# One query and key projection over exchanged halves, copied to both halves of the partitions by ScalarE

## What is computed

```python
x = _ln(x, ln1_w, ln1_b)                      # x: 8 batches of 512 tokens, 256 wide
qk = _silu(x @ Wqk.T + bqk)                   # 64 wide
v = _silu(x @ Wv.T + bv)                      # 512 wide
heads = qk[..., None, :] * gamma + beta       # four heads out of the one qk
quad_q, lin_q, quad_k, lin_k = map(_rope, (heads[..., i, :] for i in range(4)))
# _rope(h): x1, x2 = the two halves of h (32 wide each)
#           concatenate([x1 * cos - x2 * sin, x2 * cos + x1 * sin])
quad_att = einsum(quad_q, quad_k) / G + bias  # within groups of 64 tokens
lin_kv = einsum(lin_k, v) / n                 # over a batch
out = gate * (relu(quad_att)**2 @ v + lin_q @ lin_kv)
```

## Time and profile before

| | us |
|---|---|
| median of 3 runs | 1041.61 |
| lowest, highest | 1039.89, 1043.02 |
| profiled execution, its own time | 1043.68 |
| span of the profiled execution | 1041.6 |
| PE busy | 956.5 (92%) |
| DVE busy | 732.5 (70%) |
| ACT busy | 542.7 (52%) |
| attention block (until the experts' first instructions) | 347 |

### The profile page before, as it was taken

The page is one execution under the profiler, slowest core; times in us unless marked ns, Lnnn a source line. Parts: engine busy times, 40 slices in busy tenths (PEclk is TensorE's granted clock), DMA queues, the critical chain, the costliest instruction groups (busy, mean ns, idle before and its releaser), DMA issues.

```text
span 1041.6 us, 17866 instructions
## 1 busy us (share of the span) xinstructions
PE 956.5 (92%) x6060; PEld 846.2 (81%) x6060; DVE 732.5 (70%) x1671; ACT 542.7 (52%) x956; POOL 258.6 (25%) x246
## 2 busy tenths in 40 slices
PE   4979999999997899968999999999999999999971
PEld 3767788788876799957999999999999989999861
DVE  6697878787875663235666666666666678998596
ACT  5535555655455444433555555555555566666425
POOL 0050000000000037770111111112221156665551
PEclk9989999999998999998999999999999999999976
DMA  4424436533233734524344333344334436555706
GB/s 159 111 102 112 114 85 167 150 102 76 81 127 113 233 127 140 182 90 167 123 148 139 120 122 122 128 154 144 133 133 131 143 123 209 189 195 196 241 22 222
DMA packets 77426, 145.23 MB, mean 139 GB/s; under 512 B 10146, under 2 KB 61343, under 8 KB 70848
## 3 DMA queue, kind: packets, MB, share of 16 engines
q1 hardware_dynamic: 66864, 124.06, 37.4%
q0 software_dynamic: 6816, 16.86, 4.6%
q10 hardware_dynamic: 3696, 3.67, 1.0%
HBM read 99.59 MB, written 45.76 MB: 140 GB/s over the span
## 4 chain that ended last, share of the span: by engine, by line
PE 42%; DVE 9%; POOL 7%; issue 4%; DMA 2%; ACT 1%; DVEq 0%; SPq 0%; POOLq 0%
PE bank L1450 20%; PE bank L1491 20%; POOL slot_rows L1091 6%; DVE s_hl L1373 2%; PE bank L1476 2%; DMA k_wstage<-wall 1%; PE bank L1447 1%; DVE k_wpj1l L1301 1%; DVE s_wpj0l L1301 1%; DVE s_rows L1343 1%; DMA s_rows<-expert_results 1%; DVE s_mst L1351 1%; DVE s_acc L1331 0%; ACT s_h L1157 0%; DMA s_xb<-slot_rows 0%
## 5 line engine op out<-in xcount | busy, mean ns | idle before, releaser
L1157 ACT ACTIVATE s_h<-bank,k_bfc 128x512 f32<-128x512 f32 (+1 forms) x248 | 155.6, 627 | 273.5 <-PE bank L1491 243.4
L1373 DVE TENSOR_TENSOR s_hl<-s_h,s_hh 128x512 fp32r<-128x512 f32 (+1 forms) x248 | 168.1, 679 | 184.5 <-ACT s_hh L1161 183.5
L1098 POOL DMA_INDIRECT expert_results<-s_y,s_dest x78 | 85.7, 1099 | 322.5 <-ACT s_y L1138 305.7
L1491 PE MATMUL bank<-k_uh,k_wfc1h 128*128 128x512 f32 (+1 forms) x480 | 151.0, 364 | 1.2 <-DVE k_uh L1370 0.7
L1161 ACT ACTIVATE s_hh<-s_h 128x512 fp32r<-128x512 f32 (+1 forms) x248 | 141.4, 570 | 10.7
L1450 PE MATMUL bank<-k_wpj1l,s_hh 128*128 128x256 f32 x464 | 130.8, 282 | 1.5 <-DVE s_hl L1373 1.5
L1450 PE MATMUL bank<-k_wpj1h,s_hh 128*128 128x256 f32 x464 | 130.5, 281 | 0.0
L1450 PE MATMUL bank<-k_wpj1h,s_hl 128*128 128x256 f32 x464 | 130.4, 281 | 0.0
L1450 PE MATMUL bank<-s_wpj0l,s_hh 128*128 128x256 f32 x384 | 109.1, 284 | 7.7 <-DVE s_hl L1373 7.7
L1450 PE MATMUL bank<-s_wpj0h,s_hh 128*128 128x256 f32 x384 | 109.2, 284 | 0.0
L1450 PE MATMUL bank<-s_wpj0h,s_hl 128*128 128x256 f32 x384 | 108.9, 284 | 0.0
(11 more groups left out here) (284 smaller groups left out, 2288.5 us busy)
## 6 DMA issues: line engine op xcount, KB each, us to landing
k_wstage<-wall SPq DMA_DIRECT2D x50, 1024.0 KB, 5.2
slot_rows<-s_empty SPq DMA_DIRECT2D x6, 1677.0 KB, 11.5
s_xb<-slot_rows SPq DMA_DIRECT2D x15, 516.0 KB, 4.0
s_rows<-expert_results SPq DMA_DIRECT2D x12, 512.0 KB, 7.4
s_x_in<-x SPq DMA_DIRECT2D x8, 512.0 KB, 3.5
s_x_res<-x SPq DMA_DIRECT2D x8, 512.0 KB, 11.0
x_rows<-s_x SPq DMA_DIRECT2D x8, 512.0 KB, 2.8
x_parts<-s_x1h SPq DMA_DIRECT2D x8, 512.0 KB, 2.6
```

Of the source, the lines that this page charges most:

```text
L1098: pool.indirect_dma_start(YY, bass.IndirectOffsetOnAxis(dest[i][:, t:t + 1].bitcast(U32), 0), y[:, t, :], None, bounds_check=2 * N - 1, oo ...
L1157: nc.scalar.activation(h[j % 2][:, cols], b[:, cols], ACT.Gelu_apprx_tanh, bias=bfc[w][:, j:j + 1]).then_inc(h_ev, 1)
L1373: tt(hl[j % RING][:, cols], h[j % 2][:, cols], hh[j % RING][:, cols].bitcast(F32), ALU.subtract).then_inc(hl_rd, 1)
L1491: last = mm(b[:, cols], wfc[w][ws][:, c, rows_], xs[i][:, c, cols], start=c == 0 and p == 0, stop=c == KD - 1 and p == 2)
```

## The change

The projection is made once: its 128 columns are qk (partitions 0 to 63) and halves(qk) (partitions 64 to 127), in bank 4. ACT reads each half of the partitions and writes it to both halves of `qk[:, s, :]`: four activations of 64 partitions each, in place of two of 128. DVE's first rope multiplication waits for the first two of them, its second for all four. The one product now waits for both things for which the two products waited: `u_ml` (bank 4's former reader) and `x1T_ev` (bank 5's). Bank 5 keeps only its other uses. The weights shrink from 512 to 256 values a partition, so their load and their two splitting instructions shrink too.

```diff
-        wqk, wv, wg, wo = (pair(n, s) for n, s in (("wqk", [P, 2, KD, P]), ("wv", [P, KD, E]),
+        wqk, wv, wg, wo = (pair(n, s) for n, s in (("wqk", [P, KD, P]), ("wv", [P, KD, E]),
...
-        raw_qk = raw[:, 2048:2560].rearrange("p (s k n) -> p s k n", s=2, k=KD)
+        raw_qk = raw[:, 2048:2304].rearrange("p (k n) -> p k n", k=KD)
...
                 if main:
+                    act.wait_ge(q_mm, b + 1)
                     for s in range(2):
-                        act.wait_ge(q_mm, 2 * b + s + 1)
                         need(act, qkr_rd, 2 * (b - 1) + s + 1)
-                        nc.scalar.activation(qk[:, s, :], bank[4 + s][:, :], ACT.Silu,
-                                             bias=vec[:, BQK + s:BQK + s + 1]).then_inc(q_ev, 1)
+                        src = slice(s * QK, (s + 1) * QK)
+                        for dst in (slice(0, QK), slice(QK, P)):
+                            nc.scalar.activation(qk[dst, s, :], bank[4][src, :], ACT.Silu,
+                                                 bias=vec[src, BQK + s:BQK + s + 1]).then_inc(q_ev, 1)
...
                     for s in range(2):
-                        dve.wait_ge(q_ev, 2 * b + s + 1)
+                        dve.wait_ge(q_ev, 4 * b + 2 * s + 2)
...
                 if main:
-                    for s in range(2):
-                        if at(0):
-                            pe.wait_ge(wl_rd, 2)
-                        if s == 0:
-                            need(pe, u_ml, 4 * b)
-                        else:
-                            need(pe, x1T_ev, 2 * (c - 1) + 2)
-                        for k in range(KD):
-                            last_i = three(bank[4 + s][:, :], wqk[0][:, s, k, :], wqk[1][:, s, k, :], xTh[:, k, :], xTl[:, k, :],
-                                           k == 0, k == KD - 1)
-                        last_i.then_inc(q_mm, 1)
+                    if at(0):
+                        pe.wait_ge(wl_rd, 2)
+                    need(pe, u_ml, 4 * b)
+                    need(pe, x1T_ev, 2 * (c - 1) + 2)
+                    for k in range(KD):
+                        last_i = three(bank[4][:, :], wqk[0][:, k, :], wqk[1][:, k, :], xTh[:, k, :], xTl[:, k, :], k == 0, k == KD - 1)
+                    last_i.then_inc(q_mm, 1)
...
     wqk = f[A + "Wqk"].T
-    wqk = np.stack([chunks(np.concatenate([w, w], 1)) for w in (wqk, halves(wqk))], 1)
+    wqk = chunks(np.concatenate([wqk, halves(wqk)], 1))
```

## The result

The changed kernel takes 1052.93 us (median of 4 runs, 1049.41 to 1054.31) against 1040.75 of the kernel before, measured beside it (4 runs, 1039.2 to 1043.02): a ratio of 1.0099, 95% interval 1.0082 to 1.0116. It is slower by some 10 to 12 us where the prediction had it 1.5 us faster. The two profiled executions, 1052.98 and 1043.68, are 9.3 us apart; spans 1051.1 and 1041.6.

What follows compares the result with a forecast made beforehand. PE was taken as the bound, with a second loop 1.49 us behind. Gains of 0.8 and 1.6 us less 0.85 for PE's clock gave 1.55 us, so 1040.1 us, with an 80% range of 1036.4 to 1043.2.

Steps and rivals of the forecast that it cites:

- What bounds the kernel: Attention steps: PE first, period 35.3 us, with a second loop through ACT and DVE only 1.49 us shorter in step 4.
- the loop: Each step: scores, gate, kv, transposes, xT, shift, x1, Silus, rope, heads, scores; slack 1.49 us, 0.74 in step 2.
- The four Silus: ACT, each step: four 64-partition Silus bounded from 1.14 to 2.28 us, taken as 2.28, at a pitch of 0.57.
- the 1.1: DVE's heads, each step: 1.1 us later because the second rope multiplication waits for the fourth Silu.
- G: Gain with which step 2 begins, from steps 0 and 1: 0.8 us.
- rival 2: Step 1: POOL's and DVE's order flips; 1041.0 us (chance 0.16), or 1037.8 if the load lands later (0.08).
- The clock: PE in step 2: a 1.76 us wait may bring the half clock, costing 0 to 1.67 us; 0.85 taken.
- rival 3: PE's clock falls in each of steps 2 to 7, losing 1.67 us each: 7.6 us slower, 1049.2; chance 0.10.
- The sum: Whole kernel: G 0.8 plus 1.6 through step 7 makes 2.4 us, less 0.85 for the clock: 1.55 us gained.
- Rival 1: PE is the only bound, so all 11.2 us of removed projection work come off: 1030.4 us; chance 0.08.
- What would show it: Trace signs: Silus 0.57 apart, PE idle at keys 0.9 us (1.8 in step 2), period 34.9, unchanged order in step 1.

Runs made afterwards that it cites:

- the four full-width Silus: Changed kernel with four Silus of all 128 partitions, the second of each pair into a scratch tile, values wrong: 1042.2 us, ratio 1.001 of the kernel before.
- The dead product: Changed kernel with the projection computed a second time into bank 5, read by nobody: 1097.9 us, ratio 1.0032; the changed kernel beside it 1103.09.
- three Silus: Changed kernel with one 128-partition and two crossed 64-partition Silus, ahead of x1, and POOL's splits in six pieces: 1072.56 us, ratio 0.9814 of before.
- the splits in pieces: POOL's four weight splits made six, started behind DVE's shifts of steps 2 to 7: changed kernel 1086.97 us (0.9942), kernel before 1083.06 (0.9907).

## Why the prediction was wrong, step by step

**What bounds the kernel: right.** There are two bounds 1.49 us apart. 33.81 plus what is put on the loop gives the measured periods of the four full-width Silus (35.03) and, within 0.05 of its step 6, of the changed kernel.

**The four Silus: the first step that failed.** I bounded them from 1.14 to 2.28 us and took the upper end; they took 2.83, beyond it. "Half the partitions save nothing" was true of the duration, but I priced them at the pitch of full-width ones, 0.57, and these four also lose the overlap, so each costs 0.71. The trace of before showed it in a place that I read past: in step 4 of the earlier trace rows the copy of 64x512 takes 0.63 us, and in step 0 the copies stand at 33.88 (64x512) and 34.53, 0.65 apart for 0.63 of duration. The second rope multiplication started 179.60 - 176.77 = 2.83 us behind the first Silu in place of 1.31, and the last head 2.81 behind that in place of 2.71: the 1.1 is 1.62 us. Against a slack of 1.49 that changes the sign: in place of 0.39 us gained in each of steps 3 to 6, 0.13 is lost. The experiment with full-width Silus kept the 0.57 and showed no loss and no gain (1042.2 against 1041.94). Even there the heads came 1.22 us later and not 1.1, and the period was 35.03 and not 34.9: the term was a little too small at the pitch that I had assumed, too.

**G, the gain of steps 0 and 1: wrong.** I took 0.8, it was -2.13. In step 0 ACT was to reach kT 1.0 earlier; with Silus 1.7 us longer it reached it 0.06 earlier (34.47 against 34.53), so PE waited for it 1.17 in place of 0.53 us and gained 0.06. With full-width Silus it was there at 33.50, the 1.0 earlier of the forecast. For the same reason the load that starts POOL came only 0.12 us earlier and not 1.0, while DVE's heads came 0.57 later (57.34 against 56.77): 0.69 later by POOL's split, where I had 0.2. POOL went first. Both margins were smaller than the error in the Silus' price, so **rival 2 became the case**. The Trainium skill's rule on the shared port ("SBUF — State Buffer", section "Who interferes with whom": issue order decides who blocks) agrees with the rows: the first head took 2.40 us behind POOL and 0.75 ahead of it. Its size was underestimated too: I had kv end 1.1 later, and the u product came 2.13 later. The other 1.0 is the gate: PE's clock, at its lower level from 61.99, stayed there until 79.06 and not 71.64, and the gate took 8.02 us (73.91 to 81.93) in place of 6.99 (69.13 to 76.12). I had no term for that. The kv product did escape its half clock (3.60 us against 5.37), as written.

**The clock: between forecast and rival 3.** I gave the wait in step 2 the middle, 0.85 us, and rival 3 all six steps. It fell in three, steps 2 to 4, behind waits of 1.90, 1.33 and 1.25 us at the keys, and not in steps 5 to 7 behind 1.25, 0.88 and 0.29. At full clock the period is 35.5; in steps 3 and 4 it was 37.1 and 37.0, so each fall costs about 1.6 us, near the 1.67 of the prediction. For steps 2 to 4 that is about 4.7 us. The dead product is the test: the same Silus and the same order in step 1 with PE kept busy show 1.00 in all of steps 2 to 6, in both of its traces.

**The sum with the measured sizes.** Step 1: 2.2. Step 2: 2.33, of which some 1.6 is the clock and the rest the loop, which there had only 0.74 of slack. Steps 3 and 4: 1.77 and 1.70, 3.2 of it the clock. Steps 5 and 6: 0.7. Step 7 and the tail give back 0.7. That is the 7.9 of the ledger; the mechanisms were in the text, but for the longer half clock of step 1, and the case that happened is the one in which rival 2 and half of rival 3 come together with an error in a price. I had treated them as separate cases.

**Rival 1** (PE as the only bound, all 11.2 us) failed. With the added work off the loop and the splits out of step 1 the change gives 7.4 us of it, with three Silus 10.5 (the latter with a step 0 at full clock).

**What would show it.** The Silus are 0.71 apart and not 0.57; 575 and 576 stand 1.6 later behind `shift`, not 1.1; PE's wait at the keys is 1.90, 1.33, 1.25, 1.25, 0.88 and not 1.8 and 0.9; the u product waits for kvl in no step; the order in step 1 is not the same; the period is 37 and then 35.5, not 34.9.

**What stays open.** Whether the lost overlap comes of the 64 partitions or of the changing start (above). Which wait lets the clock fall: behind 0.93 us or less at the keys it never fell in these traces, from step 2 on, and behind 1.42 or more always; but it also stayed up behind 1.51 us ahead of the kv product in step 1 of the four full-width Silus, and behind 2.25 ahead of the transposes at 343.32 in the changed kernel, so the length of the wait alone does not decide. Between 0.93 and 1.42, 1.17 us did it in step 0 of three traces (the changed kernel on the third chip, and the two with its four Silus and the splits in pieces) and not in two (the first trace of the changed kernel, and the one with the Silus ahead of x1), and 1.25 and 1.33 to 1.37 did in some and not in others. Why the clock fell in steps 3 and 4 in one trace of the changed kernel and in step 0 in the other was not found.

The profiled run of the four full-width Silus was 2.9 us ahead of before at the experts, while its median is level; its runs spread over 6.7 us, and only the fastest has a trace. Each kernel but the changed one and the one with the dead product has a single trace, so how often the clock falls in one step or another is not known.

## What to carry to other kernels

Work taken off the busiest engine is a gain only as far as the loop behind it has slack; beyond that it is idle time, and idle time on PE can cost its clock, so that the kernel ends slower than with the useless work left in. Before trading such work for instructions on a loop that is 1.49 us from binding, first take those instructions off the loop, and see that no collision waits behind it: with the Silus ahead of x1 alone the kernel was level with before, with the splits moved as well the same change brought 0.7% (7.4 us). Price an added instruction by its distance to its neighbours in a row of the same shape and the same sequence of partitions, not by the distance of another kind. And where the sign of a step depends on an order decided by 0.06 us, remove the collision rather than estimate it: that alone brought 0.9% here, more than the change.

## What the runs showed of the hardware that I had not expected

- A ScalarE activation over 64 partitions of 512 f32 is as long as one over 128 (0.68 us). Four in a row that start at partitions 0 and 64 by turns do not overlap: pitch 0.70 to 0.71 us, against 0.57 for 128 partitions. One from partition 0 behind a full one that starts there too did overlap, by 0.10 us.
- PE's clock fell to its lower level behind some single waits of 1.17 to 1.9 us in a stretch that was otherwise full, and 6 unread matmuls a step kept it at 2.4 GHz in steps 2 to 6: 1097.9 us with them, 1103.09 without.
- In step 1 the scores started 4.8 us later (71.90 against 67.13) when POOL's split came 0.42 us ahead of DVE's first head, and not 0.27 behind it. All traces of kernels with four half-width Silus and whole splits have the late order, those with full-width Silus the early one.
